# Two batches through four attention layers: long chains cut into parts, and stretches without an attention

## What is computed

```
L0: h += attn(LN h, LN h); h += attn(LN h, ctx)       16 heads of 64; softmax
    h += (lin * gelu(gate)) @ w_ff2                    feed-forward of 512
L1: out = LN(softmax(LN(text) LN(audio)^T) audio @ W_out + h)   one head of 128
L2: x += mha(h, h); x += mha(LN x, ctx); x += gelu-MLP          16 heads of 8, biases
L3: x += attn of rotated, unit-length q and k over ctx          16 heads of 8, RMS norm
```

## Time and profile before

| | us |
|---|---|
| median of 3 runs | 2313.88 (2312.68 to 2314.91) |
| the profiled execution | 2315.39 |
| its span, first to last instruction | 2313.5 |
| mean granted TensorE clock, as a share of full speed | 0.92 |

### The profile page before, as it was taken

One profiled execution on the slowest core, in us unless ns is written; L12 is line 12 of the kernel. 1 busy time (PEld: TensorE's weight loads), 2 busy tenths in 40 slices (PEclk: granted clock), 3 DMA queues, 4 the chain that ended last, 5 costly groups with the idle time before them and its releaser, 6 DMA issues.

```text
span 2313.5 us, 40668 instructions
## 1 busy us (share of the span) xinstructions
PE 1852.8 (80%) x13184; PEld 1406.7 (61%) x13184; DVE 1335.2 (58%) x3255; ACT 1205.2 (52%) x2794; POOL 365.3 (16%) x835
## 2 busy tenths in 40 slices
PE   1889886787689988777768998777768899877777
PEld 1677665554477766555557776555546776665554
DVE  2667565763267756576226765666624675656742
ACT  1556443457355654355645555345655565543565
POOL 0000003421100001332200000233210000023321
PEclk7999998999799999898979999989888999998999
DMA  5000000000000000000000000000000000000000
GB/s 131 7 1 1 1 1 1 1 1 1 18 1 1 1 1 1 1 2 1 1 18 1 1 1 1 1 1 1 1 9 9 1 1 1 1 1 1 1 1 6
DMA packets 23858, 13.68 MB, mean 6 GB/s; under 512 B 9202, under 2 KB 23157, under 8 KB 23637
## 3 DMA queue, kind: packets, MB, share of 16 engines
q1 hardware_dynamic: 23636, 10.92, 1.9%
HBM read 9.86 MB, written 1.05 MB: 5 GB/s over the span
## 4 chain that ended last, share of the span: by engine, by line
PE 59%; DVE 22%; ACT 9%; issue 5%; DMA 2%; POOL 1%; SPq 1%; POOLq 0%; ACTq 0%; DVEq 0%
PE heads_out L922 9%; DVE nmax L1678 6%; PE turned L545 5%; PE chain_bank L605 4%; PE heads_out L861 3%; PE scores L475 3%; PE scores L477 3%; PE scores L476 3%; PE chain_bank L545 3%; PE turned L848 3%; PE heads_out L545 2%; PE scores L827 2%; PE chain_bank L475 2%; PE queries_m L475 2%; ACT L1064 2%
## 5 line engine op out<-in xcount | busy, mean ns | idle before, releaser
L1678 DVE TENSOR_REDUCE nmax<-scores 128x1 f32<-128x512 f32 (+1 forms) x768 | 517.3, 685 | 155.4 <-PE scores L477 76.0
L1204 ACT ACTIVATE probs<-scores,nmax 128x256 f32<-128x256 f32 (+1 forms) x512 | 292.9, 577 | 43.1 <-DVE nmax L1678 42.3
L1220 ACT ACTIVATE probs_t<-turned 128x512 f32<-128x512 f32 x384 | 219.9, 597 | 121.1 <-PE turned L848 114.9
L922 PE MATMUL heads_out<-probs_t,v 128*64 128x256 f32 (+1 forms) x2560 | 266.1, 402 | 3.2 <-ACT probs_t L1230 3.2
L1805 POOL TENSOR_TENSOR rstd<-var_eps,minus_half 128x2 f32<-128x2 f32 x80 | 58.1, 726 | 1261.1 <-DVE var_eps L1349 1213.5
L545 PE MATMUL turned<-ident,probs 128*128 128x128 f32 x1536 | 239.5, 279 | 5.1 <-ACT probs L1204 4.6
L545 PEld LDWEIGHTS turned<-ident,probs 128*128 128x128 f32 x1536 | 192.9, 145 | 46.2 <-ACT probs L1204 11.1
L1880 POOL CAST q_mask<-q_t 32x256 fp32r<-32x256 f32 x384 | 159.8, 416 | 287.6 <-DVE q_t L1402 89.4
L848 PE MATMUL turned<-shifted_mask,k_t 128*128 128x256 f32 x768 | 177.2, 321 | 26.7 <-ACT probs_t L1220 22.1
L827 PE MATMUL scores<-k_t,q_mask 128*128 128x256 f32 (+1 forms) x512 | 173.5, 396 | 24.8 <-DVE nmax L1678 12.2
L1005 ACT ACTIVATE t_hi<-queries_m 128x256 fp32r<-128x256 f32 (+1 forms) x256 | 98.0, 383 | 176.1 <-PE queries_m L477 175.1
(11 more groups left out here) (333 smaller groups left out, 3997.5 us busy)
## 6 DMA issues: line engine op xcount, KB each, us to landing
out_t<-ctx_dram SPq DMA_DIRECT2D x8, 192.0 KB, 2.7
v<-wqt_dram SPq DMA_DIRECT2D x2, 512.0 KB
wo<-wo_dram SPq DMA_DIRECT2D x2, 512.0 KB, 5.3
x<-x_dram SPq DMA_DIRECT2D x8, 128.0 KB, 2.6
y_dram<-x SPq DMA_DIRECT2D x8, 128.0 KB, 2.3
v<-wkt_dram SPq DMA_DIRECT2D x1, 512.0 KB
probs_t<-wv_dram SPq DMA_DIRECT2D x1, 512.0 KB
wff<-wff_dram SPq DMA_DIRECT2D x1, 512.0 KB, 6.7
```

What stands on the lines that cost most here:

```text
L922: last = nc.tensor.matmul(O[rows, 0:S], stationary, probs_t[:, h % ph.slots, kb, :], start=(kb == 0), stop=(kb == ph.kb - 1))
L1204: last = nc.scalar.activation(out, src, ACT.Exp, bias=nmax[:, h * QB + qb:h * QB + qb + 1], accum_out=sums[:, qb, h:h + 1])
L1220: nc.scalar.activation(half_probs[:, v % ph.halves, :, :], bank[:, :].rearrange("p (k q) -> p k q", k=2), ACT.Exp).then_inc(sem["attention ...
L1678: nc.vector.tensor_reduce(out, src, AX.X, ALU.max, negate=True).then_inc(sem["attention_max"], 1)
```

## The change

It writes another order for the small layers. In the large ones the plan is as before, except that end of stream 1 now stands beside self0 of stream 0 of the next segment, ahead of start of stream 1. In the small layers the order of attentions is self2(0), cross2(0), self2(1), cross2(1), l3(0), l3(1) where it was self2(0), self2(1), cross2(0), cross2(1), l3(0), l3(1); the number is the stream. mid1 of stream 1 and mid3 of stream 0 are cut into three parts, mid3 of stream 1 and start of stream 0 into two (`CUTS`). Three phases without an attention (48 units each, `BETWEEN`) hold two lanes of chains that alternate:

1. mid2(0), and mid1(1) from its text projection to the L1 output;
2. mid2(1), and mid3(0)'s MLP;
3. end(0) and the rest of start(0), and mid3(1) from its MLP to its turned queries.

Beside self2(0) stand only the first nine steps of mid1(1) and keys2(0); beside cross2(0) mid1(1)'s last 15 and keys3(0); beside self2(1) the first eight steps of mid3(0) and keys2(1); beside cross2(1) mid3(0)'s last part and keys3(1); beside l3(0) the first eight steps of mid3(1) and start(0)'s ctx; beside l3(1) nothing. A second set of scratch tiles serves mid2, end(0) and start(0). It lies in `probs`, which the small layers don't use. After x1_t, text, s0, s1 and pv the next step must be of the same lane (`HELD`), because these leave a bank filled for it. end(1) uses the bank Y alone. The segments are first, second, loop (2 times), last and over; SP loads ctx and x at different places.

```diff
-PAIR = [("self0", 0, [[("start", 1)]]), ("self0", 1, [[("mid0", 0)]]), ("cross0", 0, [[("mid0", 1)]]),
-        ("cross0", 1, [[("mid1", 0)]]), ("self2", 0, [[("mid1", 1)], [("keys2", 0)]]),
-        ("self2", 1, [[("mid2", 0)], [("keys2", 1)]]), ("cross2", 0, [[("mid2", 1)], [("keys3", 0)]]),
-        ("cross2", 1, [[("mid3", 0)], [("keys3", 1)]]), ("l3", 0, [[("mid3", 1)]])]
+def large(before):
+
+    return [("self0", 0, [before + [("start", 1)]]), ("self0", 1, [[("mid0", 0)]]), ("cross0", 0, [[("mid0", 1)]]),
+            ("cross0", 1, [[("mid1", 0)]])]
+
+def small(chain, behind):
+
+    return [("self2", 0, [[("mid1", 1, 0)], [("keys2", 0)]]),
+            ("", 0, [[("mid2", 0)], [("mid1", 1, 1)]]),
+            ("cross2", 0, [[("mid1", 1, 2)], [("keys3", 0)]]),
+            ("self2", 1, [[("mid3", 0, 0)], [("keys2", 1)]]),
+            ("", 0, [[("mid2", 1)], [("mid3", 0, 1)]]),
+            ("cross2", 1, [[("mid3", 0, 2)], [("keys3", 1)]]),
+            ("l3", 0, [[("mid3", 1, 0)]] + chain),
+            ("", 0, [[("end", 0)] + behind, [("mid3", 1, 1)]]),
+            ("l3", 1, [])]
 SEGMENTS = {
-    "first": [("", 0, [[("start", 0)]])],
-    "loop": PAIR + [("l3", 1, [[("end", 0), ("start", 0)]]), ("", 0, [[("end", 1)]])],
-    "last": PAIR + [("l3", 1, [[("end", 0)]]), ("", 0, [[("end", 1)]])],
+    "first": [("", 0, [[("start", 0, 0), ("start", 0, 1)]])],
+    "second": large([]) + small([[("start", 0, 0)]], [("start", 0, 1)]),
+    "loop": large([("end", 1)]) + small([[("start", 0, 0)]], [("start", 0, 1)]),
+    "last": large([("end", 1)]) + small([], []),
+    "over": [("", 0, [[("end", 1)]])],
 }
-LOOPS = B // STREAMS - 1
+LOOPS = B // STREAMS - 2
+CUTS = {("mid1", 1): ("text", "wout"), ("mid3", 0): ("m3_t", "rmshat"), ("mid3", 1): ("m3_t",), ("start", 0): ("stats",)}
+SECOND_SCRATCH = {("mid2", 0), ("mid2", 1), ("end", 0), ("start", 0)}
+HELD = ("x1_t", "text", "s0", "s1", "pv")
+BETWEEN = 48
...
 def planned(lanes, units):
...
+    waiting, plan = sorted(steps, key=lambda at: at[0]), []
+    while waiting:
+        held = plan and plan[-1][2][2] in HELD
+        at, lane, step = waiting.pop(next(k for k, w in enumerate(waiting) if not held or w[1] == plan[-1][1]))
+        plan.append((max(at, plan[-1][0] if plan else 0), lane, step))
+    return [(at, step) for at, _, step in plan]
...
-    ("start", 1): {"ctx": 0.8, "stats": 4, "ln1": 0.64, "split": 6.25, "v0": 1.6, "v1": 4, "v3": 2.5},
+    ("start", 1): {"ctx": 2, "stats": 4, "ln1": 0.64, "split": 6.25, "v0": 1.6, "v1": 4, "v3": 2.5},
+    ("end", 1): {"t0": 0.6, "t1": 0.6, "nat_t": 0.6, "wo": 1.5},
...
+        small = [probs[:, n // 2, n % 2 * S:(n % 2 + 1) * S] for n in range(4)]
+        blocks_of = lambda t: t.rearrange("p (b n) -> p b n", b=QB)
+        scratch = []
+        for n, tiles in enumerate(((xhat, nat_q, xz, sb("heads_nat", [P, QB, D])),
+                                   (blocks_of(small[0]), blocks_of(small[1]), small[2], blocks_of(small[3])))):
...
+            def next_first(b):
+
+                for content in ("qt0", "qt1"):
+                    sp.wait_ge(sem[filled(("mid3", 0, content))], FILL["mid3", 0, content])
+                load_ctx(0, b + STREAMS)
+                store(0, b)
+                load_x(0, b + STREAMS)
...
             with sp.Fori(0, LOOPS) as b:
                 enter("loop")
-                load(1, b * STREAMS + 1)
-                store(0, b * STREAMS)
-                load(0, b * STREAMS + 2)
+                load_ctx(1, b * STREAMS + 3)
                 store(1, b * STREAMS + 1)
+                load_x(1, b * STREAMS + 3)
+                next_first(b * STREAMS + 2)
                 segment_over()
```

More of the change, by code:

```diff
@@ L203, in bank_name @@
     spare = content in ("g1", "l1", "s1", "p1", "qkv1", "up1", "kv1", "qt1", "kt1", "t1")
+    if (chain, s) in (("mid1", 0), ("end", 1)):
+        return "chain"
     if chain in ("mid2", "mid3"):
@@ L207, in bank_name @@
         spare = s == 0 and content in ("v1", "v3")
-    return "spare" if spare and (chain, s) != ("mid1", 0) else "chain"
+    return "spare" if spare else "chain"
 def filled(key):
@@ L304, in run_rounds @@
     ending = iter(())
+    work, ahead = {}, {}
     for (phase, ps, lanes), plan in zip(SEGMENTS[segment], PLAN):
[L306 to L310, removed]
+        units = PHASES[phase, ps].steps if phase else BETWEEN
+        for lane in lanes:
+            for name, s, *part in lane:
+                if part in ([], [0]):
+                    work[name, s] = chain(name, s)
+                    ahead[name, s] = next(work[name, s], None)
+        emitted = attention(PHASES[phase, ps]) if phase else iter((None,) * (BETWEEN + 1))
         next(emitted)
@@ L456, in program, with scratch_of @@
         segments_over = ctx.enter_context(nc.semaphore("segments_over"))
+        def scratch_of(chain, s):
+            return scratch[(chain, s) in SECOND_SCRATCH]
         def bank_of(key):
@@ L522, in segment_end @@
             eng.wait_ge(segments_over, ends)
+            if isinstance(ends, int):
+                eng.drain()
         block = ctx.enter_context(nc.Block())
@@ L591, in turn_heads @@
                     pe.wait_ge(sem[bank_read((chain, s, content))], FILL[chain, s, content])
[L592 removed]
+                turn_tokens((chain, s, "nat_t"), scratch_of(chain, s).heads_nat, QB)
                 yield "wo"
@@ L996, in _ @@
             segment("first", 1)
+            segment("second", 2)
             with pe.Fori(0, LOOPS) as b:
-                segment("loop", b + 2)
-            segment("last", LOOPS + 2)
+                segment("loop", b + 3)
+            segment("last", LOOPS + 3)
+            segment("over", LOOPS + 4)
         @block.scalar
```

103 lines of the change are left out of this document (62 added, 41 removed).

## The result

The changed kernel takes **2476.03 us** (median of 4 runs, 2469.13 to 2477.16), the kernel before 2313.28 (4 runs): a ratio of 1.070, 95% interval 1.068 to 1.072. I had forecast 2332 us, in a range of 2285 to 2380. The sign was right, the size was not: 163 us were lost where 18 were forecast.

A forecast was written before the change was run, and what follows sets the result against it. The prediction took waits in a fixed order, chain steps holding attention units in the same queues, as the bound. Per-pair terms: L2 +6, l3 +15, last pair +7, pass ends -19, self0 +9; total +18, 2332 us (2285 to 2380).

The forecast's parts named there:

- Both signs of being wrong: Forecast wrong if the three gaps take under 78 or over 95 us a pair, or self2(0) stays above 38 us.
- self2 of the first batch: First small-layer attention, keeping nine steps of mid1 and keys2: 32 us (27 to 38) in place of 63.
- The ends of the passes: From the last head to the next pass: moving end of the second batch away saves 19 us in all.
- self2 of the second batch: This attention, with 10 chain steps beside it in place of 19: 27 us (25 to 31), where it took 31.
- cross2 of the first batch: This attention changes one set of late chain steps for another: 46 us as before.
- First gap: Stretch without attention, mid2 and mid1's middle part: 27 us with 0.5 to the next scores, bounds 19 and 35.
- Second gap: Stretch without attention, mid2 and mid3's middle: 22.5 us, between 16 and 26, with little overlap.
- Third gap: Stretch with end and start of the first batch beside mid3's rest: 35 us, then 2.5 to first exp; last pair 27.
- (1): Whole kernel: the two sides nearly cancel, a little slower; 2319 to 2350 us, chance 0.38.
- (2): In the gaps, two chains hide each other nearly fully: 2274 us, halfway 2303; chance 0.33.
- (3): In the gaps the granted clock falls to half speed: up to +24 us per pair, at half that 2380; chance 0.17.
- (4): DVE stands behind the wait for x: 5 us more per third gap, 4 in self0; 2359 us, chance 0.07.

The follow-up runs named there:

- e_warm1: Changed kernel with one unused PE transpose after each of the 48 units of every stretch without an attention; 2438.96 us.
- e_floor: Changed kernel with mid1(1)'s first part moved from self2(0) into the first stretch, mid3(0)'s from self2(1) into the second; 2508.04 us.
- e_ends: Changed kernel with small layers in the old order, keeping end(1) beside self0, split loads and five segments; 2300.93 us, ratio 0.9915 to the kernel before.

## Why the prediction was wrong

Per pair, L2 was forecast at 199.9 us; it took 233.9 in the changed kernel in the mean of four pairs, and 222.6 in e_warm1, with a clock of 1.00 in its two stretches. Before: 199.7. Both signs of being wrong that I had set came true: the three gaps of the second pass take 102.8 us together (over 95; up to 2.5 of them stand beside the gaps in my sum), and self2 of the first batch stays at 39.5 (over 38).

- **The ends of the passes**: -19 forecast, -18.5 measured; last exp to first exp of self0 went from 17.5, 17.3 and 13.5 us to 8.0, 13.0 and 6.7. Right, and so was the branch that is left: the pass over it keeps 13.0 where the others keep 8.0 and 6.7. Beside self0, +9 forecast: from its first to its last exp it takes 1.3, 3.2 and 4.8 us longer in the three passes with end beside it, 9.3 in all. That the large layers as a whole grew by only 3.8 is luck: the rest, which the change left alone, varies by more than that from run to run. The first pass is 4.0 us shorter here, and takes 270.6 to 277.3 us in runs with the same large layers.
- **self2 of the second batch**, "27 us (25 to 31)": 31.7, and 30.7 in e_warm1 at 0.89. **The first failed step.** I took its length for a function of the number of steps beside it and took off 4 us for nine steps fewer. The floor with no such step is 28.7 in e_floor: mid2 had cost 1.2 us there as measured, so hardly anything was there to be saved.
- **self2 of the first batch**, 32 (27 to 38): 39.5. The same step failed from the other side: the nine steps kept are the dear ones (14.0 of the 35 us that all 37 cost). The two table loads, for which my term had nothing, are some 2.5 of it; the stall in front of the attention's scores, part of it at half clock, is in the trace, but its whole price isn't measured. I had summed PE pieces only.
- **cross2 of the first batch**, "one set of late chain steps for another: 46 us as before": 51.0, of which e_warm1 gives 0.9 back. The two sets weren't alike: 1.9 us apart on DVE, which bounds the part with the maxima, and 2.8 us at the end, where PE ran at 0.76 and not at 1.00.
- **cross2 of the second**, 46: 47.1 to 49.7. Near.
- **First gap, 27 us (19 to 35)**: 35.5. Two errors cancelled at full clock. In turn the lanes take 30.9, not the 35 I added up from an attention's surroundings, and alternating hides 1.6 of that, not 8. That gives 28 to 29, near my 27, by luck; the clock does the rest, 7.3 us. **The second failed step** is the same for all stretches: that nothing of the clock stands in the sum.
- **Second gap, 22.5 (16 to 26)**: 28.5 (26.0 to 30.1 in the four pairs), of which 3.5 is the clock.
- **Third gap, 35 and 2.5 to the first exp**: 38.8 in the pass shown, 36.1 to 38.8 in the three pairs with start, 30.4 in the last, against 29.5. Right, DMA wait included: DVE's statistics wait 3.81 us for x. l3(0) took 25.8 (25), l3(1) 21.3 (22). That the l3 stretch still cost 17 us more than forecast is a **fault of the baseline**: the 79.5 and 69.7 us of before ran from the first scores to the last head, my new sum from first exp on; like for like before had 75.7 and 65.9, which is 15 of the 17 us.

The sum of these, over four pairs: L2 131 us above the forecast, l3 17, the large layers 5 below. Of the 131 the clock is 45 by e_warm1 (11.3 a pair). The other 86 are the attentions, at the clocks that they had there (0.83 to 0.89), and what the two gaps take at full clock; how much of the 86 is clock inside the attentions isn't measured.

**The rivals.** (1), my forecast, fell with the two steps above. (2), lanes that hide each other, is refuted: 1 to 3 us in L2. (3), the clock, was right in kind and near in size: I gave it 48 us, runs show 37 in the whole kernel. The Trainium skill (TensorE: Matmul & The Clock Gate, HAM oscillation) says that short bursts of matmuls between waits fall back to the slow clock; the trace agrees, with 0.57 over the first stretch against 1.00 in e_warm1. But in this kernel it is a quarter of the loss, and half the clock isn't twice the time: 7.3 us on 28.2, since only PE's part of the chain slows down; DVE is busy 11.6 us there at either clock. (4), the wait for x, is in the third gap's own price. What I had no rival for is C: that the attentions keep their length when the chain beside them goes, so that the removed cost is small while the added one is whole. Its observation was in the earlier trace rows: self2(1) with 19 steps beside it ran at 31 us and a clock of 1.00, and the earlier trace rows alone can't say whether 31 is steps or floor. Whoever has only such a row has to keep "nearly all of it is floor" as a case with a chance of its own.

Still open: what the low clock inside the attentions costs, in the stall of self2(0) and at the end of cross2(0) above all, and whether idle PE work in e_ends would gain anything; neither was tried.

## What to carry to other kernels

Before a chain is moved out from beside a loop, measure that loop without it: the cost removed is the difference to its floor (here 1 and 4 us, by the estimate above up to 2 more each at equal clocks, for the 17 steps of mid2), not a share by steps, while the cost added is the whole latency (20 us). Two dependent chains that alternated on the same in-order queues hid 1 to 3 us of each other here, not the shorter one; what had filled their waits was independent work, the attention. And in a stretch of bare latencies TensorE's clock fell, which was worth up to a fifth of its length; the piece of such a change that removes waits without making a bare stretch (end beside self0 and the earlier load of ctx, 0.9% faster) is to be taken alone.

## What was not expected of the hardware

Idle matmuls paid for themselves: 48 transposes of a 128x128 tile in each stretch, some 6 us of PE time by the difference in busy time between the runs with one and two (18.7 and 24.8 us in the first stretch), made the kernel 37 us faster; twice as many 19 us faster, and four times as many 64 us slower. The third stretch shows the limit: its clock stayed at 0.78 with one and at 0.87 with two, and its length went up by 0.6 and 0.8 us. DVE's wait for x is in it as before, 3.9 us in e_warm1; that this wait is the reason wasn't tested. And the attention that follows a slow stretch got only 0.9 us shorter when its mean clock rose from 0.76 to 0.83. Between its first and last maximum nothing changed at all (36.8 and 36.7 us, DVE 88% busy); the 0.9 us came behind.
